# A dilation over 121 taps: seven left chains in PSUM, more DMA adds, clamps on GpSimd, and rows of m pitched 260

## The reference

```python
x = x + dilation(_gn(x), kernel, R)          # R = 5
x = x + _L1_conv_ref(_gn(x), ...)            # projection, 3x3 convolution, norm, GELU, offsets, bilinear sampling
```

```python
acc = jnp.maximum(acc, sl - kflat[:, idx][None, :, None, None])   # 121 times
```

## Time and profile before

| | us |
|---|---|
| median of 3 runs | 10762.84 (10760.06 to 10778.29) |
| profiled execution | 10759.57 |
| its span | 10757.7 |

### The profile page before, as it was taken

How to read it: one execution, slowest core, us unless ns; L and a number is a source line. 1 busy time by engine, 2 the same in 40 slices (tenths; PEclk the granted TensorE clock), 3 DMA queues, 4 the chain that set the end, 5 groups by cost and what they waited for, 6 DMA issues and landing times. The chain is left out here.

```text
span 10757.7 us, 72949 instructions
## 1 busy us (share of the span) xinstructions
PE 8270.0 (77%) x17056; PEld 3131.6 (29%) x17056; DVE 10336.3 (96%) x5749; ACT 9666.7 (90%) x6995; POOL 9024.2 (84%) x2890
## 2 busy tenths in 40 slices
PE   1777777777777777777777777777777777887888
PEld 0222222222222222222222222222222223333333
DVE  7999999999999999999999999999999998998999
ACT  2999999999999999999999999999999996776666
POOL 2888888888888888988888888888888885666898
PEclk9999999999999999999999999999999998998999
DMA  7777666676767677677666767667767764343666
GB/s 299 138 139 138 136 133 133 135 136 135 137 135 138 136 138 139 134 139 139 136 137 136 139 137 138 136 134 139 139 137 137 138 119 140 153 160 156 249 254 247
DMA packets 408034, 1618.63 MB, mean 150 GB/s; under 512 B 21920, under 2 KB 128416, under 8 KB 358048
## 3 DMA queue, kind: packets, MB, share of 16 engines
q0 software_dynamic: 243712, 971.69, 50.8%
q1 hardware_dynamic: 163872, 642.05, 16.1%
HBM read 397.22 MB, written 201.33 MB: 56 GB/s over the span
## 5 line engine op out<-in xcount | busy, mean ns | idle before, releaser
L482 POOL TENSOR_TENSOR m<-m,u 128x2048 f32<-128x2048 f32 x1536 | 6567.5, 4405 | 509.0 <-ACT m L576 507.7
L678 DVE SCALAR_TENSOR_TENSOR acc_a<-m,kt,acc_a 128x2048 f32<-128x2048 f32 x1472 | 3466.4, 2355 | 48.9 <-POOL m L482 3.4
L544 PE MATMUL chain<-dx,mats 128*128 128x512 f32 x6144 | 2950.4, 614 | 520.6 <-ACT chain L594 520.0
L544 PE MATMUL chain<-dx,neg_ident 128*128 128x512 f32 x4608 | 2325.6, 644 | 867.8 <-ACT chain L594 867.7
L678 DVE SCALAR_TENSOR_TENSOR acc_a<-t,kt,acc_a 128x2048 f32<-128x2048 f32 x896 | 2108.9, 2354 | 22.8
L544 PE MATMUL chain<-u,mats 128*128 128x512 f32 x3072 | 1570.2, 635 | 561.2 <-ACT chain L594 560.8
L576 ACT ACTIVATE m<-dx,gap_l 128x2048 f32<-128x2048 f32 x960 | 1921.5, 2002 | 59.2 <-POOL dx L444 34.3
L544 PEld LDWEIGHTS chain<-dx,mats 128*128 128x128 f32 x6144 | 1094.8, 191 | 2397.7 <-ACT chain L594 1387.3
L678 DVE SCALAR_TENSOR_TENSOR acc_a<-u,kt,acc_a 128x2048 f32<-128x2048 f32 x704 | 1655.9, 2352 | 13.7
L594 ACT ACTIVATE chain<-chain,gap_r 128x1024 f32<-128x1024 f32 x1536 | 1626.2, 1088 | 46.1 <-PE chain L544 40.0
L453 POOL DMA_DIRECT2D t<-u x896 | 1235.6, 1448 | 469.8 <-ACT t L576 464.0
(11 more groups left out here) (144 smaller groups left out, 6543.0 us busy)
## 6 DMA issues: line engine op xcount, KB each, us to landing
t<-u POOLq DMA_DIRECT2D x896, 1059.0 KB, 8.7
u<-x_dram SPq DMA_DIRECT2D x32, 2688.0 KB, 24.9
xw<-x_scratch SPq DMA_DIRECT2D x65, 1152.0 KB, 7.3
hw<-h_scratch SPq DMA_DIRECT2D x66, 1024.0 KB, 9.3
xt<-x_dram SPq DMA_DIRECT2D x32, 2048.0 KB, 14.4
x_scratch<-x SPq DMA_DIRECT2D x64, 1024.0 KB, 4.0
h_scratch<-h SPq DMA_DIRECT2D x32, 2048.0 KB, 7.3
out_dram<-res SPq DMA_DIRECT2D x64, 1024.0 KB, 4.9
```

What stands on the lines that cost most here:

```text
L482: nc.gpsimd.tensor_tensor(m[j % MP][:], m[j % MP][:], rows, ALU.add).then_inc(m_ready, 1)
L544: added = nc.tensor.matmul(chain[h][:, r:r + 2, :], weight, src[:, top:top + 2, dj:dj + W], start=False, stop=True, skip_group_check=True)
L678: nc.vector.scalar_tensor_tensor(out=acc_a[:], in0=src, scalar=k_base, in1=acc_a[:], op0=ALU.subtract, op1=ALU.max).then_inc(a_done, 1)
```

## The change

Seven rows (0 to 6) get a left chain; before, rows 0 to 2 had a left and rows 3 to 5 a right one. The pairs by DMA go from 14 to 16, the pairs whose relu ScalarE writes from 24 to 17, and seven pairs (1, 5, 8, 12, 15, 18, 22 of the 24 that GpSimd adds) get their first operand by a clamp on GpSimd. The rows of the buffers m are pitched 260 elements, for 256. The clamp applies min first and max second for both sides. The four order strings are new. `dilation_taps` itself is unchanged.

```diff
-CHAINS = ((0, "left"), (1, "left"), (2, "left"), (3, "right"), (4, "right"), (5, "right"))
-NPOOL, NDMA = 24, 14
-
-CLAMPED = ()
+CHAINS = ((0, "left"), (1, "left"), (2, "left"), (3, "left"), (4, "left"), (5, "left"), (6, "left"))
+NPOOL, NDMA = 17, 16
+
+CLAMPED = (1, 5, 8, 12, 15, 18, 22)
...
-ACT_ORDER = "r0x1r01rx01b0r1x0r10r10u10x1r0r10rx10r1r0x1r0x10x10r10r10xr1r0r1x01r01x0r01xx10r0r10x10r10r1r1"
-PE_ORDER = "010101010101010101010101010101010101010100110010101011"
-DVE_ORDER = "mm0s1sysmmy0s1mmymsmm0y1msymmymy0s1smsmymymm0my1ymssym0ym1ymm"
-POOL_ORDER = "tittitittidtttitittiittditttiittititittt"
+ACT_ORDER = "rx0r10x10b10x1r0r10x10x10r1r01x01r01r0x1r0x10r10u10x1r0x10x10x10r1r01x01x01r0r1x0x10r10r101"
+PE_ORDER = "01010101010101010101010101010101010101010101010101010101"
+DVE_ORDER = "mm0y1mymmsy01mmymys0m1mmysms0y1ymmmym01yysmmy0m1mmyymmy0m1my"
+POOL_ORDER = "cittiticttitcittittitdcittictititictdittittictitt"
...
-        m = [sb(f"m{s}", [P, CR, W]) for s in range(MP)]
+        m = [sb(f"m{s}", [P, CR, W + 4])[:, :, 0:W] for s in range(MP)]
...
-                    first, second = (ALU.max, ALU.min) if right else (ALU.min, ALU.max)
+                    gap = gap_l[:, g, at_col:at_col + 1]
+                    low, high = (gap, FAR) if right else (-FAR, gap)
...
-                    nc.gpsimd.tensor_scalar(m[j % MP][:], dx[s][:, top:top + CR, lo:lo + W],
-                                            gap_l[:, g, at_col:at_col + 1], FAR if right else -FAR,
-                                            first, second).then_inc(m_clamped, 1)
+                    nc.gpsimd.tensor_scalar(m[j % MP], dx[s][:, top:top + CR, lo:lo + W], high, low,
+                                            ALU.min, ALU.max).then_inc(m_clamped, 1)
```

More of the change, by code:

```diff
@@ L46, in passed @@
     engine.sem_inc(turns, 1)
-CHAINS = ((0, "left"), (1, "left"), (2, "left"), (3, "right"), (4, "right"), (5, "right"))
-NPOOL, NDMA = 24, 14
-CLAMPED = ()
+CHAINS = ((0, "left"), (1, "left"), (2, "left"), (3, "left"), (4, "left"), (5, "left"), (6, "left"))
+NPOOL, NDMA = 17, 16
+CLAMPED = (1, 5, 8, 12, 15, 18, 22)
 MP, TP = 4, 4
-ACT_ORDER = "r0x1r01rx01b0r1x0r10r10u10x1r0r10rx10r1r0x1r0x10x10r10r10xr1r0r1x01r01x0r01xx10r0r10x10r10r1r1"
-PE_ORDER = "010101010101010101010101010101010101010100110010101011"
-DVE_ORDER = "mm0s1sysmmy0s1mmymsmm0y1msymmymy0s1smsmymymm0my1ymssym0ym1ymm"
-POOL_ORDER = "tittitittidtttitittiittditttiittititittt"
+ACT_ORDER = "rx0r10x10b10x1r0r10x10x10r1r01x01r01r0x1r0x10r10u10x1r0x10x10x10r1r01x01x01r0r1x0x10r10r101"
+PE_ORDER = "01010101010101010101010101010101010101010101010101010101"
+DVE_ORDER = "mm0y1mymmsy01mmymys0m1mmysms0y1ymmmym01yysmmy0m1mmyymy0m1my"
+POOL_ORDER = "cittiticttitcittittitdcittictititictdittittictitt"
 def numbered(order):
@@ L477, in pair @@
                         pool.wait_ge(m_clamped, c * len(CLAMPED) + (CLAMPED.index(j) + 1))
-                        nc.gpsimd.tensor_tensor(m[j % MP][:], rows, m[j % MP][:],
+                        nc.gpsimd.tensor_tensor(m[j % MP], rows, m[j % MP],
                                                 ALU.add if outer > base else ALU.subtract).then_inc(m_ready, 1)
@@ L481, in pair @@
                         pool.wait_ge(m_begun, c * NRELU + (relu_pairs.index(j) + 1))
-                        nc.gpsimd.tensor_tensor(m[j % MP][:], m[j % MP][:], rows, ALU.add).then_inc(m_ready, 1)
+                        nc.gpsimd.tensor_tensor(m[j % MP], m[j % MP], rows, ALU.add).then_inc(m_ready, 1)
                 def chunk(c, s, k, w, ahead, loads):
@@ L613, in _ @@
                                         act.wait_ge(a_done, a_free(c, "m", relu_pairs[j], NPAIR, MP))
-                                        pair_relu(s, k, pool_pairs[relu_pairs[j]], m[relu_pairs[j] % MP][:]) \
+                                        pair_relu(s, k, pool_pairs[relu_pairs[j]], m[relu_pairs[j] % MP]) \
                                             .then_inc(m_begun, 1)
@@ L660, in merge @@
                             base = outer
-                        src = m[j % MP][:]
+                        src = m[j % MP]
                     elif kind == "y":
```

## The result

The changed kernel takes 10797.65 us (median of 12 runs, 10792.6 to 10807.0) where the kernel before takes 10765.32 beside it: a ratio of 1.003, interval 1.0022 to 1.0039. It is slower by 0.3%, and the forecast of 10350 with its range up to 10600 was wrong.

What follows compares the result with a forecast made beforehand. VectorE was taken to bound the dilation at 136.4 us a chunk; after the change 127.7 + 1.3 + 1.0 = 130.0, so 6.4 less over 64 chunks, 410 us, giving 10350 us, range 10250 to 10600.

Steps and rivals of the forecast that it cites:

- the price of the pair with m pitched 260: GpSimd's add of m and u in the dilation: 3.59 us taken, from ends 3.59 and 4.14 (no effect).
- The sign named for it: Sign of a wrong forecast: VectorE's wait for POOL m or DMA t more than 3 us a chunk.
- dh beside dv: Last-stage GpSimd rows: dh, inputs pitched 257, 3.60 us; dv, plain runs, 4.56; so a plain-run input costs some 0.5.
- rival 1: Pitch does nothing, pair stays at 4.14, GpSimd bounds at 138.8 a chunk: 10949 us; chance 0.19 shared with a dear-clamp rival.
- The rival's threshold: With the pair at 4.14, the changed kernel is slower than before from a clamp of 1.96 us on.
- VectorE's 127.7: VectorE's work a chunk of the dilation after the change, 127.7 us, 7.4 less than 135.1.
- my 130.0: Dilation period a chunk: 127.7 of VectorE plus 1.3 and 1.0 of waiting, 6.4 less than 136.4.
- late t: DMA transfers of t landing at 12.3 us come 1 or 2 us late; 1 us a chunk of waiting added.
- TensorE's strict order: Chain steps now run strictly one half after the other; costed at nothing, 1 us a chunk without ScalarE's cover.
- Rivals 3 and 4: Clamp about 3.1 us: 10494, chance 0.14; coupling of engines, buffers and late t costs more, period 133: 10545, chance 0.10.
- Min-then-max "costs nothing": Order of the clamp's two operations on GpSimd: costs nothing against before, since no clamp runs there.
- That two inputs can't be read faster: Skill page's shared-port floor for GpSimd's two-input operations, 4.27 us for 2048 elements, no pitch helps; not followed, dh takes 3.60.

Runs made afterwards that it cites:

- the aligned one: Changed kernel with m's rows pitched 266 and each pair's m started so its inputs are 2 elements apart modulo 4: 10359.1 us, ratio 0.9616.

## Why the prediction was wrong

- **The step that failed is the price of the pair with m pitched 260**: put at 3.59, measured 4.13, its other end: 24 x 0.54 = 13.0 us a chunk, which made GpSimd the bound. The sign named for it came: VectorE waits 380.6 us for pairs, 5.9 a chunk. I read dh beside dv as pitched against plain. Both differ in another thing too: dh's inputs are 1 element apart and so near, dv's are 257 apart, which is 1 modulo 4. In the place of "pitched or plain" the runs show the distance between the two inputs: m at 260 alternates between a cheap and a dear row as m at 256 does. The doubt was in the text (nearness), and rival 1 hung on it; its chance of 0.19, shared, was too low for a price inferred from three rows that differ in two things. In hindsight the pair's own 4.14 fits too: it is the mean of 3.8 and 4.5.
- **Rival 1 is what happened.** It gave 10949 with the clamp at 2.3. The clamp's price was too high, 1.93 measured, which took 2.6 us a chunk off the error of the pair; with it rival 1 gives 99.4 + 13.5 + 23.3 + 0.5 = 136.7 a chunk, 10782. The DMA issues (1.25, not 1.21) make up what is left to 137.1. The rival's threshold, slower than before from a clamp of 1.96 on, had left out its own 0.5 us of waiting; with it the threshold is 1.89, and 1.93 lies above.
- **VectorE's 127.7 was right.** Busy time fell by 444 us with the stage's last 6.6 us counted (four merges of 2.355 less two halves of 1.28, 64 times: 439). Its waits shown above come to 580 us, 9.1 a chunk, which with 127.7 gives 136.8 of the 137.1.
- **The rest of the forecast was right once GpSimd fitted.** With the pair at 3.8 the list is 24 x 3.79 + 13.5 + 19.4 + 3.9 = 127.8, or 128.4 with issues at 1.25, and the period 130.2 for my 130.0. That the two agree so closely is partly luck: GpSimd is level with VectorE there and not 2.2 under it, and VectorE's 2.3 us of waiting (56.6 + 49.6 + 29.7 + 9.8 + 1.6 = 147.3 in all) are not all those of the sum, since late t cost VectorE 9.8 us in all and not 1 a chunk. TensorE's strict order, put at nothing, shows in ScalarE's waits for it (78.4 us before, 252.4 in the changed kernel, 125.9 in the aligned one), but hardly in VectorE's for the chains (43.7, 94.2, 49.6). Rivals 3 and 4 did not come about: no wide loss by the coupling showed.
- **Min-then-max "costs nothing"** was right against before, where no clamp ran, and missed what the edit is for: the other order is 5.2 us dearer a clamp.
- **That two inputs can't be read faster** was the ground on which rival 1 would have won by a rule. The pitch of 260 brought nothing, but not for that reason: 3.60 and 3.8 us were measured with other distances. By the Trainium skill's page GPSIMD Engine Reference (section 2.1), whose 2.5 cycles an element make, as an estimate, 4.27 us, neither could occur; the measurements decide. The same page of the Trainium skill gives 4497 ns for this add (section 3.1), which agrees with the dear class here, 4.50 to 4.52.

## What to carry to other kernels

When one engine is relieved, add up the lists of the others at prices that the trace shows for exactly these operands; a price inferred from a neighbouring row deserves a short measurement or an even chance. On GpSimd, the distance between the two inputs is part of the shape: here a tile pitched like its partner, started so that the distance is 2 or 3 modulo 4 elements, saved 0.34 us of 4.13 on each add, and it paid only where GpSimd was the bound.

## What the runs showed of the hardware

- GpSimd's two-input add of 128x2048 float32 takes 3.60 us for inputs -5 to +6 elements apart (first less second), else, at the distances tried, 3.8 at 2 or 3 modulo 4 and 4.5 at 0 or 1. Why is open: no run told a reading width from a bank.
- GpSimd's TENSOR_SCALAR of the same size takes 1.97 us with min then max and 7.15 with max then min. Other pairs of operations weren't tried, and why the order counts is open.
- A VectorE that merges one SBUF tile into PSUM cost GpSimd's adds nothing that shows (25.40 for 25.36 us over six).
- Issuing one DMA of 1059 KB takes 1.25 us of GpSimd's time in the changed kernel, where it has no slack, and 1.21 in the kernel before.
